# Graph transformer layer: the fourteen q and k jobs placed one pair of edge groups sooner in TensorE's order

## What is computed

```python
aggr = segment_sum(xn[src], dst) / maximum(counts, 1)       # graph
gnn = aggr @ W_l.T + xn @ W_r.T + b_r
q, k, v = split(xn @ Wqkv.T + bqkv)                         # 8 heads of 32
qn = normalize(q * scale) * scale * temperature             # attention, a second-order
kn = normalize(k) * scale                                   # expansion: no softmax
y = 0.5 * (qn.kn)**2 + scale**2 * (qn.kn) + scale**4        # weights of v, then / their sum
x = x + gnn + y_out @ Wproj.T + bproj
x = x + chosen_expert(gelu(layernorm(x) @ W1 + b1))         # 8 experts, one for each node
```

## Time and profile before

| | us |
|---|---|
| median of three runs | 259.33 |
| the three runs | 257.41, 259.45, 259.33 |
| the profiled execution, its time | 257.58 |
| its span, first to last instruction | 255.5 |
| PE busy | 238.2 (93%) |
| DVE busy | 147.9 (58%) |
| ACT busy | 144.0 (56%) |

### The profile page before, as it was taken

How to read it: one execution, slowest core, us unless ns; L and a number is a source line. 1 busy time by engine, 2 the same in 40 slices (tenths; PEclk the granted TensorE clock), 3 DMA queues, 4 the chain that set the end, 5 groups by cost and what they waited for, 6 DMA issues and landing times.

```text
span 255.5 us, 4722 instructions
## 1 busy us (share of the span) xinstructions
PE 238.2 (93%) x1428; PEld 149.5 (58%) x1429; DVE 147.9 (58%) x424; ACT 144.0 (56%) x218; POOL 33.1 (13%) x63
## 2 busy tenths in 40 slices
PE   7799889989998989999999999999899999999990
PEld 2347557555554544433348887575365578888880
DVE  2987999999999956991114556911800243333220
ACT  3699665999999984899972014444024323332000
POOL 7008300000000005600000000000360000000331
PEclk9999999999999999999999999999999999999998
DMA  4960000000000000069950000030033000000111
GB/s 128 286 214 3 0 4 3 3 6 0 5 3 3 3 5 3 0 236 423 425 236 4 0 0 0 3 122 38 9 91 113 0 1 3 0 1 3 34 35 34
DMA packets 6031, 15.82 MB, mean 62 GB/s; under 512 B 2725, under 2 KB 3784, under 8 KB 4724
## 3 DMA queue, kind: packets, MB, share of 16 engines
q1 hardware_dynamic: 4576, 13.43, 14.4%
q0 software_dynamic: 1280, 1.31, 2.0%
q10 hardware_dynamic: 144, 0.66, 0.6%
HBM read 14.08 MB, written 1.30 MB: 60 GB/s over the span
## 4 chain that ended last, share of the span: by engine, by line
PE 61%; ACT 26%; DVE 7%; DMA 2%; issue 1%; POOL 0%; DVEq 0%
ACT mem L512 22%; PE ps L1218 16%; PE ps L1156 7%; PE ps L1038 7%; PE ps L1202 6%; PE ps L1059 5%; PE ps L1118 4%; PE ps L1186 3%; PE ps L953 3%; PE ps L1107 2%; PE ps L1109 2%; DMA edges_sb<-in_edges 2%; DVE qk_sb L727 1%; DVE mem L675 1%; PE ps L1088 1%
## 5 line engine op out<-in xcount | busy, mean ns | idle before, releaser
L512 ACT ACTIVATE mem<-ids_m,half_src 125x628 bf16<-125x628 f16 x96 | 69.8, 813 | 5.4 <-DVE half_src L649 3.2
L953 PE MATMUL ps<-mem 125*128 125x501 bf16 x180 | 50.8, 374 | 4.4 <-issue 2.9
L675 DVE TENSOR_SCALAR mem<-node_ids,dst_f 125x628 bf16<-125x628 f16 x160 | 54.5, 412 | 0.0
L1218 PE MATMUL ps<-mem 128*125 x192 | 41.6, 379 | 0.0
L955 PE MATMUL ps<-mem 125*128 125x126 bf16 x180 | 39.3, 219 | 0.0
L1218 PEld LDWEIGHTS ps<-mem 128*125 128x125 f32 x192 | 36.0, 188 | 5.3
L953 PEld LDWEIGHTS ps<-mem 125*128 x180 | 17.6, 98 | 26.8 <-issue 10.3
L581 ACT ACTIVATE qk_sb<-ps,sc_col 125x626 f32<-125x626 f32 (+1 forms) x40 | 28.6, 778 | 3.7 <-PE ps L1038 3.7
L678 DVE TENSOR_SCALAR mem<-ids_m,src_f 125x628 bf16<-125x628 f16 x64 | 26.4, 412 | 0.0
L630 ACT COPY mem<-mem 128x1000 f32 x8 | 8.2, 1031 | 19.8 <-PE ps L1218 19.8
L1038 PE MATMUL ps<-mem 32*125 32x313 f32 (+1 forms) x160 | 19.1, 472 | 0.2 <-DVE mem L754 0.2
(11 more groups left out here) (199 smaller groups left out, 280.2 us busy)
## 6 DMA issues: line engine op xcount, KB each, us to landing
mem<-in_wd SPq DMA_DIRECT2D x8, 1024.0 KB, 13.2
w_sb<-in_w SPq DMA_DIRECT2D x1, 1024.0 KB, 8.6
vz<-in_bd SPq DMA_DIRECT2D x1, 1000.0 KB
wqkv_sb<-in_w_qkv SPq DMA_DIRECT2D x1, 768.0 KB, 4.2
x_all<-in_x ACTq DMA_DIRECT2D x1, 640.0 KB, 4.6
row<-rows_sorted SPq DMA_DIRECT2D x1, 579.7 KB
wlr_sb<-in_w_lr SPq DMA_DIRECT2D x1, 512.0 KB, 5.8
bqk_all<-in_b_qk SPq DMA_DIRECT2D x1, 256.0 KB, 5.0
```

The source lines that it names most:

```text
L512: ins = nc.scalar.activation(oh[:, g % OHB, 0, j, :], ids_m1[:, :], ACT.Sign, bias=half_src[:, g * GC + j:g * GC + j + 1])
L675: ins = nc.vector.tensor_scalar(oh[:, g % OHB, 1, j, :], node_ids[:, :], dst_f[:, col:col + 1], None, ALU.is_equal)
L953: mm(psf[:, bass.ds(tile * BANK, TW + 1)], node_of, oh[:, buf, 0, j, 0:TW + 1], start=False, stop=False, skip_group_check=True)
L1218: ins = mm(ps[0:TP, 4 + n % EB, 0:C], hT_step[:, n % EB, k, :], wd_sb[:, bass.ds(e, 1), k, :], start=(k == 0), stop=(k == KH - 1))
```

## The change

```diff
-        FIRST = 4
-        assert NG == 2 * NP and NG == FIRST + 2 * JOBS
+        FIRST = 2
+        LAST = NG - FIRST - 2 * JOBS
+        assert NG == 2 * NP and LAST >= 2
...
                 mm(ps[:, 7, 0:hi - lo], blk[:, :], uq[:, hg, lo:hi], start=True, stop=True).then_inc(b7_full, 1)
                 pair(FIRST // 2 + JOB_N + j)
+            for n in range(NP - LAST // 2, NP):
+                pair(n)
```

## The result

The changed kernel takes 261.95 us in the median (four runs, 261.18 to 262.74) against 259.37 for the kernel before in the same comparison (257.41 to 259.45). The ratio is 1.0115 with a 95% interval from 1.0065 to 1.0166: slower, by about 1%. The profiled execution took 261.18 us with a span of 259.1, where that of before had 255.5.

The account below looks back on a forecast made before the run. PE, nearly full, is held by evictions at fixed times. A pair and gap behind N0 (3.55 us) plus N1's wait (0.3), less N3's filled wait (0.61), gave +3.3: 262.6 by the median, taken as 262.0; range 259.2 to 264.0.

Parts of the forecast that it names:

- The start: p0 to p3: M sooner, T0 held to 41.9 by DVE's eviction of M, PE idle 2.5 us, p2 2.64 us later.
- The middle: p2 to N0: p10 ends at 80.2 to 80.5, N0 waits for U3's eviction and starts at 80.56, as before.
- The gaps that hold T4 and U2: Gaps between pairs before p10's end: T4 and U2 now wait for evictions, adding 0.7 us together.
- The end: Behind N0: five pairs in place of four, p15 ending at 101.25 to 101.5, 3.3 to 3.5 us later.
- Behind the end: After p15: copies, scores and PE's chain shift whole, with nothing gained in cover.
- The time: Whole kernel: execution 260.9 us, 262.6 by the median of the runs; 262.0 taken.
- B: Rival behind N0: less lost, within 1%, +1.6 us if PE takes no wait on ACT there; chance 0.14.
- C: Rival at the end: faster by 1.1 us, p15 directly behind p14, if N2's eviction is ready by p13's end; chance 0.05.
- D: Rival at p2: PE's clock falls behind the new 2.5 us wait, +2.3 to +2.7 us on top of A, the forecast; chance 0.06.

Follow-up runs that it names:

- last_four: Kernel before with only N0 to N3 one pair sooner; stage +3.58 us to the kernel before, ratio 1.0171.
- after_m_evicted: Changed kernel with DVE evicting M two groups sooner, behind group 5; stage +2.99 us to the kernel before, ratio 1.0121.
- after_n_evicts: Changed kernel with ACT evicting N0 to N2 two groups sooner, DVE's order untouched; stage +2.58 us to the kernel before, ratio 1.0128.
- after_all_evicts: Changed kernel with evictions of M and U0 to U3 on DVE and N0 to N2 on ACT two groups sooner; stage -0.02 us to the kernel before, ratio 1.0008.
- first_ten: Changed kernel with N0 to N3 back at their old places, M to U3 still sooner; stage +3.43 us to the kernel before, ratio 1.0103.
- only_n3: Kernel before with only N3 moved, directly behind N2 and ahead of p14; stage +4.00 us to the kernel before, ratio 1.0146.

## Why the prediction was right

The mechanism held. The end of p15, which is what the sum forecast, came 3.60 us later, where the sum had 3.3 to 3.5 and an upper bound of 3.6, so the size lies at the very edge of it; the span was 259.1 where it had 258.8. Step by step:

- **The start.** T0 at 41.77 (predicted 41.9), p2 at 42.86 (42.85), idle time before T0 2.33 us (2.5). ACT's eviction of T0 at 42.45 (42.55), its gain gone by group 13, whose end is 53.08 (53.1). Right.
- **The middle.** N0 at 80.62 (80.56). Here the step was right in its number, and its reason was only half of it: the sum let p10 end at 80.2 to 80.5 and N0 wait. In fact p10 ended at 80.59 and N0 did not wait; by its row (79.87, 0.53 long) DVE's eviction had ended at 80.40. So PE's own late start and the eviction gave N0 the same time within 0.2 us, which was luck, and the profile of the changed kernel alone could not tell them apart. The runs could: without the stall, in last_four and after_m_evicted, N0 still came at 80.5 and 80.7. Two terms of p10's time were put at nothing: p3 took 4.28 us where it had taken 4.05, and the gap behind p3 was 1.14 where the gap behind p3 had been 0.88. The gaps that hold T4 and U2 grew by 0.52, less than the 0.7 given. (A pair of fifteen blocks is thus not always 4.32 to 4.64 us, nor a gap with a job always above 0.71: that with T0 was 0.49.)
- **The end.** N1 at 84.83 (84.83), p12 85.91 to 90.58 (85.96, and 90.3 to 90.6), N3 at 94.15 (94.14), p15's end at 101.58 (101.25 to 101.5). What was mis-sized are two small terms taken from the short side: from N3 to p14 it was 1.13 us, the upper of the two values given, and the gap between p14 and p15 was 0.88 in place of 0.84. p10's late end by some 0.1 us made no difference, because N1 waited for ACT all the same (0.33 us).
- **Behind the end.** Nothing is absorbed: 157.5 us in both.
- **The time.** 262.0 was predicted and 261.95 measured. That is luck, and closer than the working deserves: the sum had 260.9 for the profiled execution, which took 261.18, and the place between the two levels of the runs was a choice. The two profiled executions differ by 3.6 us and the two medians by only 2.6, because three of the four runs of before lie at its upper level and two of the four of the changed kernel do.

Of the rivals, B's condition, no wait on ACT behind N0, was not met; after_n_evicts and after_all_evicts show what it is worth, 1.10 us alone and all of it with DVE's part. C, faster, needed N2's eviction 3.8 us sooner. That did not happen. The gain it named is there, but it lies in ACT's order and not in PE's: with the eviction moved between groups 30 and 31 the kernel before got 0.98 us faster, where C had 1.1. D, the clock, was given 0.06, and its argument was wrong, though it did not decide the profiled execution. I read from the earlier trace rows that some 4 us without a matmul are what brings the clock down. first_ten has the same wait as the changed kernel, 2.31 us, and the clock fell 1.9 us after it had ended. Its price was also less than the 2.3 to 2.7 us given: p2 lost 1.66 us, of which 1.06 were left at the end of p10. The rule of the Trainium skill that was named there (TensorE: Matmul & The Clock Gate, section "HAM oscillation — how this bites in real kernels") says that work behind waits starts at the half clock, and its example has waits of some 3 to 5 us, longer than the 2.5 predicted here. Of the runs only last_four shows just that. In only_n3 and first_ten the work started at the full clock, and it fell 0.5 and 1.9 us later. The changed kernel's own profile has the wait of 2.33 us and no fall. Where the page and these runs differ, the runs decide.

## What to carry to other kernels

Where several engines keep hand-written orders and share one buffer, find for each hand-over the engine whose order holds it, and move that one; moving the producer alone puts its other work behind the wait. Before moving a small job out of the way, look at the gap with no job in it: here it was as long (0.79 us between p10 and p11 in first_ten, 0.84 to 0.88 elsewhere) as most gaps with one (0.71 to 1.04 in the kernel before). When two limits give the same time in a profile, only a run that lifts one of them tells which would be left.

## What the runs showed of the hardware that was not expected

**The clock fell behind waits of 2.3 to 3.6 us, but not each time.** In first_ten (windows: us, busy time by engine, PE clock, DMA share, GB/s) PE waited from 39.3 to 41.6, worked again, and only then was at the level of 1.2 GHz for 3.4 us, in the midst of work:

```profile
43.00:43.50 0.50, 0.50 (x6) 0.27 (x5) 0.50 (x3) 0.50 (x2) 0.00 (x0) 1.00 0.00 0
43.50:44.00 0.50, 0.50 (x4) 0.23 (x3) 0.50 (x3) 0.50 (x2) 0.00 (x0) 0.54 0.00 0
44.00:46.00 2.00, 2.00 (x10) 0.93 (x9) 2.00 (x8) 1.01 (x2) 0.00 (x0) 0.50 0.04 8
...
47.00:48.00 1.00, 1.00 (x10) 0.80 (x9) 1.00 (x5) 0.73 (x2) 0.00 (x0) 1.00 0.00 0
```

The changed kernel and after_n_evicts have a wait of the same length (2.33 and 2.31 us) and kept 2.4 GHz in their profiles. With the waits of 3.29 us (last_four) and 3.62 (only_n3) it fell both times, in last_four 0.2 us before N0 and in only_n3 0.5 us behind the start of N3.

**The same happens ahead of the stage.** PE fills its opening with matmuls of zeros and then waits for the normalised input. In five of the twelve profiles the clock fell between 10 and 15 us of the span. In only_n3, the first four projections took 3.32 us, where before they took 1.95:

```profile
10.11 1.72 PE L910 MATMUL ps<-ident,row 125*128 125x125 f32 x10 [3.27 <-DVE row L666]
11.62 3.32 PE L917 MATMUL ps<-wqkv_sb,xnT 128*125 128x512 f32 x4
```

```profile
12.00:14.00 2.00, 2.00 (x3) 0.67 (x2) 0.98 (x4) 2.00 (x5) 0.00 (x0) 0.50 0.42 133
```

The stage then began at 33.0 to 33.4 us in place of 31.4 to 32.0. The idle time ahead of the transposes goes along with it, but for one profile: it was 2.71 to 3.27 us in four of the five and 1.37 to 2.24 in the seven where the clock stayed up, yet 1.97 in last_four, where it fell too.

The later start of the stage has the size of the distance between the two levels of the times of the kernel before, 257.5 and 259.3 us, and the granted clock of each execution is on record. Of the 50 executions of that kernel beside the experiments, nine took 259.2 us or more, and their mean granted clock was 0.986 to 0.991; 38 took at most 257.93, with 0.992 to 0.998. A fall of 3.4 us to half the clock takes 0.007 off the mean of 255 us (an estimate from the lengths above). So the upper level goes with a fallen clock; where in the span it fell in those executions, no profile shows. (Of the three executions in between, that of 258.76 us had 0.987. The other two had 0.997 and spans of 255.5 and 255.8 us, so their extra time lies outside the span.)
